# Weights and context laid out on the host with axes exchanged, and a new step order in the attention stage

## The reference, cut to what matters

```python
def _L0_xattn_ref(query, kv, Wq, Wg, bg, Wkv, Wo):
    q = query @ Wq.T
    gate = jax.nn.sigmoid(query @ Wg.T + bg)
    k, v = jnp.split(kv @ Wkv.T, 2, axis=-1)
    # 16 heads of 32; feature map: where(x > 0, x + 1, exp(x))
    kv_summary = jnp.einsum('bhsd,bhse->bhde', k, v)
    z = 1.0 / (jnp.einsum('bhld,bhd->bhl', q, k.sum(axis=-2))[..., None] + EPS)
    attn = jnp.einsum('bhld,bhde->bhle', q, kv_summary) * z
    return attn * gate @ Wo.T

h = gelu(einsum('lne,he->lnh', x, proj1) + proj1_bias)      # L0_ffn
out = einsum('lnh,eh->lne', h, proj2) + proj2_bias
scores = where(mask, x @ ctx.T / sqrt(D), -1e30)            # L1_xattn
out = softmax(scores) @ ctx
act = silu(x @ gate.T) * (x @ up.T)                         # L1_ffn, per group g
out = einsum('tg,tgh->th', w_tg, act @ down.T)              # w_tg from a top-8 router
```

## Time and profile before

| | |
|---|---|
| median of 3 runs (lowest to highest) | 1939.48 us (1938.37 to 1940.64) |
| profiled execution | 1941.13 us, span from first to last instruction 1939.3 us |
| mean granted TensorE clock | 0.994 of full speed |
| busy: TensorE, VectorE, ScalarE, GpSimd | 98%, 53%, 29%, 14% of the span |
| turned f32 tiles (L844) | 1012 transposes, four to a tile |
| all-reduces on GpSimd (L777) | 8 |
| DMA | 86.99 MB, mean 45 GB/s |
| head, up to the first q projection of item 1 | 100.74 us |
| stage A ends (first `up`) | 410.5 us |

### The profile page before, as it was taken

How to read it: one execution, slowest core, us unless ns; L and a number is a source line. 1 busy time by engine, 2 the same in 40 slices (tenths; PEclk the granted TensorE clock), 3 DMA queues, 4 the chain that set the end, 5 groups by cost and what they waited for, 6 DMA issues and landing times.

```text
span 1939.3 us, 25583 instructions
## 1 busy us (share of the span) xinstructions
PE 1900.6 (98%) x10102; PEld 962.7 (50%) x10102; DVE 1035.4 (53%) x2260; ACT 559.7 (29%) x873; POOL 280.7 (14%) x277
## 2 busy tenths in 40 slices
PE   6999998999999999999999999999999999999999
PEld 4556555644444444444444444444544444444444
DVE  7688866764545453443535545554555555545422
ACT  3145423422222221112212233232222333333321
POOL 3023211111102010101100011111111111111111
PEclk9999998999999999999999999999999999999999
DMA  6013322220101111110101020101010101000000
GB/s 218 12 42 124 106 89 82 87 98 17 44 28 60 28 64 50 56 55 22 62 1 55 1 71 1 50 1 50 1 50 1 50 1 45 5 11 13 1 22 22
DMA packets 56041, 86.99 MB, mean 45 GB/s; under 512 B 9042, under 2 KB 17362, under 8 KB 55922
## 3 DMA queue, kind: packets, MB, share of 16 engines
q1 hardware_dynamic: 55922, 85.36, 13.8%
HBM read 60.17 MB, written 25.17 MB: 44 GB/s over the span
## 4 chain that ended last, share of the span: by engine, by line
PE 86%; issue 8%; DVE 3%; POOL 1%; DMA 1%; ACT 1%; POOLq 0%; SPq 0%; DVEq 0%
PE bank L835 44%; PE bank L939 16%; PE bank L1033 10%; PE bank L844 5%; PE bank L919 4%; PE bank L885 1%; PE bank L904 1%; POOL arena L802 1%; PE bank L1020 1%; PE bank L968 1%; PE bank L995 0%; DMA x_after_ffn<-arena 0%; PE bank L984 0%; PE bank L983 0%; DMA arena<-x_after_attention 0%
## 5 line engine op out<-in xcount | busy, mean ns | idle before, releaser
L835 PE MATMUL bank<-arena 128*128 128x512 f16 x4608 | 1043.4, 380 | 3.1 <-DVE arena L1286 2.3
L835 PEld LDWEIGHTS bank<-arena 128*128 128x128 f16 x4608 | 451.0, 98 | 522.7 <-issue 5.5
L939 PE MATMUL bank<-arena 128*128 128x512 f16 x1536 | 352.1, 379 | 1.2 <-DVE arena L1469 1.2
L1033 PE MATMUL bank<-arena 128*128 128x512 f16 x1152 | 264.3, 379 | 0.9 <-POOL arena L802 0.9
L1621 DVE SCALAR_TENSOR_TENSOR arena<-bank,arena 128x512 f32<-128x512 f32 x96 | 72.0, 750 | 332.1 <-PE bank L835 332.1
L939 PEld LDWEIGHTS bank<-arena 128*128 128x128 f16 x1536 | 150.1, 98 | 173.9 <-DVE arena L1469 1.7
L1467 DVE TENSOR_SCALAR arena<-arena 128x512 f16<-128x512 f32 x128 | 69.4, 543 | 305.4 <-ACT arena L1134 305.2
L1134 ACT ACTIVATE arena<-bank,arena 128x512 f32<-128x512 f32 x128 | 99.6, 778 | 457.3 <-PE bank L835 454.3
L802 POOL TENSOR_TENSOR arena<-arena 128x512 f16<-128x512 f32 x96 | 111.1, 1157 | 628.7 <-ACT arena L1171 628.7
L844 PE MATMUL bank<-arena 128*128 128x128 f32 x1012 | 150.1, 279 | 26.4 <-DVE arena L1234 14.1
L1033 PEld LDWEIGHTS bank<-arena 128*128 128x128 f16 x1152 | 112.1, 98 | 128.3 <-POOL arena L802 1.4
(11 more groups left out here) (173 smaller groups left out, 1221.9 us busy)
## 6 DMA issues: line engine op xcount, KB each, us to landing
arena<-in_L_ffn_proj SPq DMA_DIRECT2D x48, 256.0 KB, 2.9
x_after_attention<-arena SPq DMA_DIRECT2D x8, 1024.0 KB, 4.7
arena<-x_after_attention SPq DMA_DIRECT2D x8, 1024.0 KB, 5.6
x_after_ffn<-arena SPq DMA_DIRECT2D x8, 1024.0 KB, 4.5
arena<-x_after_ffn SPq DMA_DIRECT2D x8, 1024.0 KB, 6.2
arena<-in_x SPq DMA_DIRECT2D x7, 1024.0 KB, 5.4
out<-arena SPq DMA_DIRECT2D x7, 1024.0 KB, 4.2
arena<-in_L_ffn_down_proj SPq DMA_DIRECT2D x48, 96.0 KB, 2.0
```

The lines of the kernel that those rows point to most:

```text
L835: m = e.matmul(bank[b][:, :], wT[l][:, c, tile * P:(tile + 1) * P], y[h][:, c, :], start=n == 0, stop=n == NPASS - 1)
L939: m = e.matmul(bank[t][:, :], hv[h][:, 0, t * P:(t + 1) * P], w2T[l][:, j, :], start=j == 0 and i == 0, stop=j == NH - 1 and i == 2)
L1033: m = e.matmul(bank[t][:, :], hv[h][:, 0, t * P:(t + 1) * P], dnT[l][:, j, :], start=j == 0 and i == 0, stop=j == NR - 1 and i == 2)
```

## The change

The host hands over the weight matrices and a second copy of the context with their last two axes exchanged. The kernel then has no step `wturn`, `kvturn`, `ctxturn`, `cxturn` or `gwinv`. Instead:

- Wkv and the context are loaded straight into place, by two DMAs from ScalarE's queue early in the program.
- Every weight tensor has one scale of its own. q, g, o and gw are of kind "both": maximum and split from the same loaded tile, with the all-reduce in between. 1, 2, gate, up and d have a "max" and a "col" pass each. The high part is one ScalarE pass from the staging tile and the low part one VectorE pass. GpSimd no longer scales tiles.
- A bound is worked out from the tensor's maximum with a few one-element operations; there is an all-reduce for the maximum of each tensor (q, g, c, b1, o, v, 1, 2, gate, up, d, gw).
- In stage E both layouts of the context are loaded and split; `cxsplit` has two operations on each of ScalarE and VectorE.
- The head has gates of item 0 between the `kv` steps, all numden of item 0 at its end, and the splits of Wg ahead of the first `kv`.
- In stage A, `numden` moves from beside the gates to beside `out`. `attlo` moves to GpSimd (as a plain subtraction; the scale of v is now folded into numden's denominator).

```diff
-GROUPS = ([("row", "q", t) for t in range(NC)] + [("row", "g", t) for t in range(NC)]
...
+GROUPS = ([("both", n, t) for n in "qgo" for t in range(NC)]
+          + [(how, n, t) for n in ("1", "2", "gate", "up", "d") for how in ("max", "col") for t in range(SIZE[n])]
+          + [("both", "gw", 0)])
...
+        if post[0] < pre[0]:
             w = post[0]
...
+            how, name, t = GROUPS[w]
+            if how == "max":
+                post[0] += 1
+            elif name in scaled:
+                add("wsplit", w)
+                late.append(lambda: add("wlo", w))
+                post[0] += 1
+        weight_loads()
...
     for j in range(NC):
         add("q", 0, j, banks=1)
-        weights(N_O)
+        weights(2 * NC)
+    add("ctxmax")
+    add("all", "c")
+    weights_until(2 * NC)
+    add("pow", "c")
+    add("consts")
+    add("all", "b1")
...
     for t in range(4):
         add("kv", t, banks=2)
+        if t < 2:
+            for j in (2 * t, 2 * t + 1):
+                add("gate", 0, j, banks=1)
+        add("keys", t)
+        weights(N_O)
         if t > 0:
             add("kvsum", t - 1, banks=4)
-        flush()
-        add("keys", t)
         weights(N_O)
-        norms.pop(0)()
...
+        for _ in range(2):
+            norms.pop(0)()
     add("kvsum", 3, banks=4)
     add("vmax")
     add("all", "v")
-    late.append(lambda: add("pow", "v"))
+    norms.pop(0)()
+    add("pow", "v")
+    for t in range(NT):
+        add("numden", 0, t, banks=2)
+        if norms:
+            norms.pop(0)()
+        weights(N_O)
...
-    rate = [(N_B - post[0] + 2) / (7 * 13.0), N_B]
+    rate = [(N_B - post[0] + 6) / (7 * 12.0), N_B]
...
+    for b in range(1, NB):
+        norms = ln_tasks(("A", b + 1) if b + 1 < NB else ("F", 0), apart=True)
         for j in range(NC):
...
+            add("q", b, j, banks=1)
+            add("att", b - 1, j, banks=1)
+            if j > 0:
+                add("attlo", b - 1, j - 1)
+            some()
+        for j in range(NC):
+            add("gate", b, j, banks=1)
+            if j == 0:
+                add("attlo", b - 1, NT - 1)
+            for _ in range(2 if j < 2 else 1):
                 norms.pop(0)()
...
+        for t in range(NT):
+            norms.pop(0)()
+            add("out", b - 1, t, banks=1)
+            add("numden", b, t, banks=2)
+            some()
...
+    for t in range(NT + 1):
+        if t < NT:
+            add("att", NB - 1, t, banks=1)
+        if t > 0:
+            add("attlo", NB - 1, t - 1)
+            add("out", NB - 1, t - 1, banks=1)
+        some()
...
+            elif kind == "attlo":
+                _, b, t = step
+                cols = slice(t * P, (t + 1) * P)
+                w.wait_ge(a_hi, n)
+                if b > 0:
+                    w.wait_ge(o_mm, NT * b)
+                e.tensor_tensor(aT[1][:, :, cols], attw[(n - 1) % 2], aT[0][:, :, cols], ALU.subtract).then_inc(a_lo)
...
+            elif kind == "kvload":
+                e.dma_start(wkvT, wkv.rearrange("(c p) n -> p c n", p=P)).then_inc(kvn_in, 16)
+                e.dma_start(ctxT, ctx_t.rearrange("(c p) n -> p c n", p=P)).then_inc(ctx_in_s, 16)
...
+                w.wait_ge(scale_of["v"], 1)
                 for i in range(2):
-                    e.tensor_scalar(zd_v(i), v[i][:, :, P:P + HPT], 1e-6, None, ALU.add).then_inc(nd_z)
+                    e.tensor_scalar(zd_v(i), v[i][:, :, P:P + HPT], 1e-6, sc["ti"], ALU.add, ALU.mult).then_inc(nd_z)
```

More of the change, by code:

```diff
@@ L92, in make_plan @@
     load, pre, post = [0], [0], [0]
-    late = []
+    late, scaled = [], set()
     def flush():
@@ L104, in weight_loads @@
             load[0] += 1
[L106 to L115, removed]
     def weights(upto=N_D):
@@ L125, in weights @@
                 add("wmax", pre[0])
-            if how == "max" and t == SIZE[name] - 1:
-                add("all", name)
-                late.append(lambda: after_max(name))
+                if t == SIZE[name] - 1:
+                    add("all", name)
+                    late.append(lambda: after_max(name))
             pre[0] += 1
-        if pre[0] - post[0] >= 3 or pre[0] >= upto:
+        if post[0] < pre[0]:
             w = post[0]
[L132 to L136, removed]
+            how, name, t = GROUPS[w]
[6 more added lines that the diff above has]
+        weight_loads()
     def after_max(name):
         add("pow", name)
+        scaled.add(name)
+        if name in BOUNDED:
+            add("bound", name)
         if name in ("2", "d"):
@@ L165, in make_plan @@
     weight_loads()
-    for i, f in enumerate(ln_tasks(("A", 0))):
-        f()
[L168 to L171, removed]
+    norms = ln_tasks(("A", 0), apart=True)
+    for i, f in enumerate(norms):
+        f()
+        if i >= NT - 1:
+            weights(NC)
+        if i == NT - 1:
             add("kvload")
     weights_until(NC)
-    add("consts")
+    add("small")
     add("xload", "A", 1)
@@ L275, in make_plan @@
+        if b + 2 < NB:
+            add("xload", "A", b + 2)
+        else:
+            add("xload", "F", b + 2 - NB)
+    for t in range(NT + 1):
[4 more added lines that the diff above has]
+            add("out", NB - 1, t - 1, banks=1)
+        some()
+    add("xstore", "A", NB - 1)
     add("b2")
@@ L304, in both @@
             return go
-        return [L[0], both(split, L[1]), L[2], both(lambda: add("cxturn", b, banks=1), L[3]), L[4], L[5], L[6],
+        return [L[0], both(split, L[1]), L[2], L[3], L[4], L[5], L[6],
                 lambda: add("scores", b, banks=1), lambda: None, lambda: add("pturn", b, banks=1),
@@ L802, in pool_program @@
                 e.tensor_tensor(rh[1][:, 0, :], r, rh[0][:, 0, :], ALU.subtract).then_inc(m_lo)
-    all_n, k_all = {}, 0
-    for step in plan.steps:
-        if step[0] in ("all", "bound"):
-            k_all += 1
-            all_n[step] = k_all
     def dn_value(n):
@@ L852, in tensor_program @@
                 turn4(step, yn_s[(n - 1) % 2], y_turned)
-            elif kind == "wturn":
-                k = step[1]
-                how, name, t = GROUPS[k]
-                w.wait_ge(const, C_ID)
-                if how == "row":
-                    w.wait_ge(w_scaled, sum(g[0] == "row" for g in GROUPS[:k + 1]))
-                else:
-                    w.wait_ge(w_in[k % 4], w_landed[k])
-                turn4(step, stg[k % 4], w_turned)
             elif kind == "q":
```

433 lines of the change are left out of this document (131 added, 302 removed).

## The result

| | before | changed |
|---|---|---|
| median (lowest to highest) | 1939.74 us (1938.37 to 1940.64, 4 runs) | 1926.41 us (1925.13 to 1929.03, 4 runs) |
| profiled execution, span | 1941.13, 1939.3 us | 1925.13, 1923.0 us |
| first q projection of item 1 | 100.74 us | 112.37 us |
| first `up` (stage A ends) | 410.54 us | 404.40 us |
| stages F and E | 1528.8 us | 1518.6 us |

The ratio is 0.9934 (95% interval 0.9922 to 0.9946). The sign was right; 1903 and its range of 1888 to 1920 were not.

What follows compares the result with a forecast made beforehand. TensorE, busy 1900.6 of 1939.3 us, was taken as the bound. Savings 16.3 + 3.5 + 14.1 + 12.4 = 46.3 less losses 8.3 + 1.3 = 9.6 gave 36.7 net, 1904.4 profiled, 1903 us median; range 1888 to 1920.

Steps and rivals of the forecast that it cites:

- Prices on PE: TensorE start-to-start costs: projection 2.59 us, turned tile 0.43 to 0.44, numden block 0.90; an attention item 38.2 us.
- Up to 0.75 us: Attention's output phase: VectorE's 128x512 operations take at most this each, so a block needs 3.9 us against PE's 3.93.
- F and E stages otherwise keep their order: Loop over W1 and W2 and expert stage: no new waits costed, removed weight transposes save 16.3 us there.
- the second pass's loads at "nothing": Second pass over "1", "gate" and "up": 40 more loads of 256 KB, four ahead of use, cost nothing.
- About 1 us: Attention: the `half` pow and VectorE's wait for it cost this much, covered by PE's lead of eight banks.
- The 12.4 us: Attention: saving from removing the 9.9 us stall for normalised rows and 2.5 us of lower clock after it.
- Head: Start up to item 1's first q projection: at 109.0 us, 8.3 us later than before, despite 24 fewer transposed tiles.
- The gate stall: Head: PE idles 7.8 us before gate 0, as Wg's all-reduce queues behind the fourth q add; then 2.5 us clock loss.
- the keys' stall: Head: kv(2) waits 2.1 us for kv(1)'s banks, which `keys` frees only after kvsum(0).
- the three values: Head, first q start: 23.5 us taken, 24.6 if DMA engines take turns between queues, 21.9 if served in issue order.
- Final wait: End of attention: with attlo on GpSimd the wait grows from 2.1 to 3.4 us, a loss of 1.3.
- The jam rival: Attention: GpSimd or VectorE jams, or head stalls drop the clock and x comes 1 us later; 1911 to 1930, chance 0.27.

Runs made afterwards that it cites:

- The put-back transposes: Changed kernel with four unused TensorE transposes of the identity ahead of each of 37 weight-tile splits in the loop over W1 and W2: 1939.06 us, ratio 0.9999.

## Why the prediction was wrong

- **Prices on PE: right.** In the loop passes of items 2 to 5 the output blocks start at 173.45, 212.45, 250.62 and 288.80 us, so 38.2 apart in the last two steps; 438 instructions fewer (437 forecast). The put-back transposes cost 0.44 us a tile again. Two slips did no harm. "Up to 0.75 us" takes the shortest of these rows for the longest (the median is 1.31 us), but in the changed kernel's output phase from 212.45 us on VectorE's 128x512 passes do take 0.54 to 0.75 us. And 64 steps over 84 slots are 0.76 a slot, not 0.83; the plan adds 6 steps, and with 0.83 the two all-reduces fell where forecast.
- **"F and E stages otherwise keep their order", and the second pass's loads at "nothing": the step that failed most** (9.6 us: 6.8 of waits, 1.7 of lower clock, 0.6 at the first `down`, 0.5 not placed). PE's instructions keep their order there, but the slots of weight work shifted against the items. The forecast asked of the new loads only whether the DMA path has room (45 GB/s), not what stands behind them in SyncE's queue. Two of the five waits are settled by runs: one of these loads ahead of a store (2.0 us, 3.9 with the clock), and `half` of "d" with its changeover, which stood at 839 us, before the reload, and now falls at 850, just ahead of the statistics (2.5 us). The three small ones (2.7 us) were not tested singly. All but one go when the rows are asked for later (7.9 us).
- **"About 1 us" for `half`'s wait: a wrong size.** It was 4.03 us and 1.7 of lower clock. The text had the 7.6 us of the changeover back in hand, and gave it "PE's lead of eight banks" as cover without asking what VectorE had queued behind: a turned block that a projection's bank needed. I also named the wrong reduction for the stall before the change (bound "1"); it was the maximum of "2", with `half` behind. The 12.4 us were right as a loss to be had back, but the same reduction stayed in the program.
- **Head: 3.4 us too long.** x came 4.5 us late, not 1.6, and q started at 26.18 us, not 23.5; that is 2.7 of the 3.4. The gate stall (8.06 for 7.8) and the keys' stall (2.24 for 2.1) were right to 0.3 us. Asking for the 3 MB behind the first all-reduce gave 3.5 us back. By the rule of the Trainium skill, DMA: Bandwidth & Descriptors, section Queues, rings and completion order, that each DMA engine takes turns between the queue rows with work, I had 24.6: of the three values the nearest. The trace agrees with turns (296 packets of one queue, 298 of the other), and the 24.6 came out too early because it shared by bytes, and W_kv's packets are twice as long. By equal packets, 2.1 MB pass beside x's 1.05, which at 394 GB/s is an estimate of 5.3 us against the 4.5 measured. (The kernel before has its data on one queue, as the forecast says; 1.6 MB more are on two instruction queues.)
- **Final wait: right in size, wrong in what it was compared with.** 3.15 + 0.26 us for 3.4 forecast, and 1.4 of lower clock not forecast. The slower low half on GpSimd costs 0.5 us at the first block, as reckoned (2.64 on VectorE), but on VectorE three more blocks would wait, and the kernel is 6.3 us slower.
- **The jam rival** (0.27, 1911 to 1930) held the measured time, and partly its mechanism: an all-reduce whose way back something waits for, x 3 us later than taken, and short stalls that drop the clock. Its other part, GpSimd and VectorE in each other's way in the q phase, is not seen: the items stay 38.2 us apart. It lay outside the range because I cut it at 1920.

With four edits of the order of steps (rows and scales later, the 3 MB behind the all-reduce, the gates one block later) the kernel runs in 1902.9 us, and nothing of its arithmetic is changed. That this is the forecast's 1903 is chance: the gates' stall, which these edits take away, was in the forecast. The forecast priced the change's work and not its new waits.

## What to carry to other kernels

When work is taken out of one engine's stream, go through every loop with a fixed order and ask for each step where it now stands against the load, the store and the slow reduction next to it; a stage whose own instructions don't change can lose as much as the changed one. An engine's changeover must be priced at the steps queued behind whoever waits for it, and a short stall with the lower clock that can follow it (2.0 us became 3.9). And an experiment that gives nothing may be hiding a gain behind the next limit: the gates were worth nothing alone and 5.4 us beside the three other edits.

## What the runs showed of the chip

- **GpSimd's changeover to an all-reduce goes with DMA traffic.** In the head it took 5.57 us with quiet queues, 5.70 with traffic in its first 2 us, 9.66 with full DMA engines for 7; elsewhere in the two kernels it took 5.70 to 6.38. The way back to ordinary operations is 6.8 to 7.8 us. The traffic's part rests on one execution with full engines. The Trainium skill, GPSIMD Engine Reference, section Instruction dispatch, gives some 6 us for the first call of a freshly loaded kernel: the quiet runs agree (5.57), the busy one does not.
- **Two queues share by packets, not by bytes.** 296 packets of 1.06 MB on ScalarE's queue and 298 of 0.54 MB on SyncE's in the same 4 us. The first root came 4.5 us later with 3 MB asked for on ScalarE's queue at once, and no later with the same 3 MB behind x on SyncE's.
- **A stall's clock loss is not a constant.** The same f32 block behind the same waits took 10.04 us at a granted clock of 0.71 and 7.13 at 1.00 (2.4 GHz). In the changed kernel a stall of 1.99 us was followed by 1.7 us lost at 1.2 GHz, and one of 2.47 us by none.
